# Cross attention's value product: probabilities stationary, value columns moving

## What is computed

```python
def _attn(q, k, v):
    s = jnp.einsum('bhqd,bhkd->bhqk', q, k) * SCALE
    p = jax.nn.softmax(s, axis=-1)
    return jnp.einsum('bhqk,bhkd->bhqd', p, v)
...
ctx = _attn(qT, k.transpose(0, 2, 1, 3), v.transpose(0, 2, 1, 3))
ctx_dca = _attn(qT, k_dca.transpose(0, 2, 1, 3), v_dca.transpose(0, 2, 1, 3))
ctx = ctx + DCA_WEIGHT * ctx_dca
return ctx @ Wo + bo
```

## Time and profile before

| | |
|---|---|
| median of 3 runs | 1019.32 us (1016.58 to 1019.96) |
| the profiled execution | 1017.64 us |
| its span, first to last instruction | 1015.9 us |
| mean granted clock of PE over the span | 0.832 |
| PE busy | 675.2 us (66%) |
| DVE busy | 728.4 us (72%) |
| ACT busy | 331.4 us (33%) |

### The profile page before, as it was taken

How to read it: one execution, slowest core, us unless ns; L and a number is a source line. 1 busy time by engine, 2 the same in 40 slices (tenths; PEclk the granted TensorE clock), 3 DMA queues, 4 the chain that set the end, 5 groups by cost and what they waited for, 6 DMA issues and landing times. The chain is left out here.

```text
span 1015.9 us, 9504 instructions
## 1 busy us (share of the span) xinstructions
PE 675.2 (66%) x3066; PEld 442.1 (44%) x3069; DVE 728.4 (72%) x1418; ACT 331.4 (33%) x530; POOL 193.8 (19%) x167
## 2 busy tenths in 40 slices
PE   4418986777777354349963454999990344389997
PEld 2304543343343243335742243556550123277775
DVE  5987798999999767659653783766429886944554
ACT  4004424525350133122302324555530222423231
POOL 0000002212222000034352940000003132203342
PEclk9759999999999776569986855999995575569999
DMA  9200004555555840323632000000005000000000
GB/s 243 76 12 0 1 0 78 87 94 93 97 90 97 206 128 1 124 62 108 133 92 87 0 1 0 1 2 1 1 1 207 0 1 0 10 0 1 20 3 21
DMA packets 35746, 55.27 MB, mean 54 GB/s; under 512 B 4578, under 2 KB 23658, under 8 KB 34418
## 3 DMA queue, kind: packets, MB, share of 16 engines
q0 software_dynamic: 10960, 22.94, 12.5%
q1 hardware_dynamic: 24738, 31.73, 10.2%
HBM read 31.73 MB, written 6.16 MB: 37 GB/s over the span
## 5 line engine op out<-in xcount | busy, mean ns | idle before, releaser
L499 PE MATMUL ps<-hT,regA 128*128 128x512 f32 x256 | 116.8, 599 | 1.3 <-ACT hT L424 1.3
L669 POOL DMA_DIRECT2D yssm<-regB x32 | 38.7, 1210 | 294.6 <-DVE regB L621 210.8
L613 DVE TENSOR_TENSOR_SCAN regB<-regB 128x512 f32<-128x512 f32 x64 | 74.9, 1212 | 5.0 <-DVE regB L608 0.5
L510 PE MATMUL ps<-regA,regC 128*128 128x256 f32 x256 | 64.8, 398 | 20.5 <-DVE regC L628 17.2
L1914 PE MATMUL ps<-regC 128*34 128x256 f32 x256 | 68.2, 389 | 11.6 <-ACT regC L1794 11.6
L499 PEld LDWEIGHTS ps<-hT,regA 128*128 128x128 f32 x256 | 49.2, 193 | 52.2 <-issue 47.7
L510 PEld LDWEIGHTS ps<-regA,regC 128*128 128x128 f32 x256 | 49.7, 199 | 39.8 <-DVE regC L628 27.1
L434 ACT ACTIVATE regC<-ps 128x512 f32<-128x512 f32 x32 | 19.1, 597 | 138.1 <-PE ps L499 138.0
L1128 POOL TENSOR_TENSOR w_lo<-regA,w_hi 128x768 fp32r<-128x768 f32 x22 | 42.4, 1932 | 100.3 <-ACT w_hi L1090 100.3
L1352 POOL DMA_INDIRECT regA<-h_rows,regA x31 | 29.5, 951 | 137.4 <-DVE regA L1572 107.1
L1266 DVE TENSOR_TENSOR regB<-regB,ps 128x512 f32<-128x512 f32 x22 | 15.1, 687 | 45.9 <-ACT regB L1108 45.9
(11 more groups left out here) (365 smaller groups left out, 1701.7 us busy)
## 6 DMA issues: line engine op xcount, KB each, us to landing
yssm<-regB POOLq DMA_DIRECT2D x32, 512.0 KB, 5.0
regB<-in_L_w SPq DMA_DIRECT2D x4, 1088.0 KB, 12.1
regA<-in_L_w SPq DMA_DIRECT2D x1, 4224.0 KB, 14.9
y_rows<-regA SPq DMA_DIRECT2D x31, 128.0 KB
regB<-in_L_w SPq DMA_DIRECT2D x1, 2176.0 KB, 13.1
regC<-in_L_W SPq DMA_DIRECT2D x2, 1024.0 KB, 5.7
x<-in_x SPq DMA_DIRECT2D x1, 1024.0 KB, 5.7
regB<-in_L_gate_pk SPq DMA_DIRECT2D x1, 1024.0 KB, 8.0
```

The lines of the kernel that those rows point to most:

```text
L499: m = nc.tensor.matmul(ps[:, 2 + 2 * (u % 2) + j, :], w[:, k * 2048 + c * P:k * 2048 + (c + 1) * P], hT[:, k, hf * HALF:(hf + 1) * HALF], ...
L510: m = nc.tensor.matmul(ps[:, t // 2, (t % 2) * D:(t % 2 + 1) * D], itm[:, u % 2, t * P:(t + 1) * P], WDv[:, c // 2, c % 2, :], start=(c == ...
L613: v.mark(nc.vector.tensor_tensor_scan(hs[:, k, :], dA[:, g % RD, k].rearrange("p b l -> p (b l)"), dBu[:, k, :], 0.0, ALU.mult, ALU.add))
L669: nc.gpsimd.dma_start(y, hc[:, g % 2], accum_op=ALU.add).then_inc(s_y, 16)
```

## The change

In `values(n)` the operands change places. For each of the two query tiles `qt` and the two key tiles `kt` a 128 keys x 128 queries block of `prob` is stationary, and the 34 columns of `vaug` move. The result has the queries on the partitions at once, in the layout that `normalize` reads. `evacuate_values` (the ACT copy), `turn_values` (the four turns), the tile `pvT` and the semaphores `s_pe` and `s_pt` go; `normalize` waits for `s_pv`.

```diff
-                    def evacuate_values(j):
-                        act.wait_ge(s_pv, j + 1)
-                        if j >= 2:
-                            act.wait_ge(s_pt, j - 1)
-                        nc.scalar.copy(pvT[0:VW, j % 2, :], ps[0:VW, 6 + j % 2, :]).then_inc(s_pe, 1)
...
-                        for kt in range(2):
-                            m = nc.tensor.matmul(ps[0:VW, 6 + j % 2, (n % 2) * S:(n % 2 + 1) * S], vaug[:, 2 * b + kt, hd, :],
-                                                 prob[:, n % 4, kt * S:(kt + 1) * S], start=kt == 0, stop=kt == 1)
+                        for qt in range(2):
+                            c0 = (2 * (n % 2) + qt) * VW
+                            for kt in range(2):
+                                m = nc.tensor.matmul(ps[:, 6 + j % 2, c0:c0 + VW],
+                                                     prob[:, n % 4, kt * S + qt * P:kt * S + (qt + 1) * P],
+                                                     vaug[:, 2 * b + kt, hd, :], start=kt == 0, stop=kt == 1)
                         if n % 2:
                             m.then_inc(s_pv, 1)
-
-                    def turn_values(j):
-                        pe.wait_ge(s_pe, j + 1)
-                        for i in range(4):
-                            m = nc.tensor.transpose(ps[:, 6 + j % 2, i * VW:(i + 1) * VW],
-                                                    pvT[0:VW, j % 2, i * P:(i + 1) * P], ident[0:VW, 0:VW])
-                        m.then_inc(s_pt, 1)
...
-                                if n >= 2 and n % 2 == 0:
-                                    turn_values(n // 2 - 1)
...
-                    turn_values(NHB // 2 - 1)
...
-                        dve.wait_ge(s_pt, j + 1)
+                        dve.wait_ge(s_pv, j + 1)
```

More of the change, by code:

```diff
@@ L1657, in stage4 @@
             rz = ar.take([8])
-            pvT = ar.take([2, 2 * S])
             nm = ar.take([2, 2, NH, 2])
@@ L1662, in stage4 @@
             (s_var, s_sd, s_h, s_hTp, s_hT, s_wk, s_w, s_v, s_q, s_qe, s_kv, s_kve, s_kb, s_qv, s_qs, s_sqi, s_sq, s_kp, s_qp, s_T, s_Te,
-             s_s1, s_mx, s_qm, s_s2, s_p, s_pv, s_pe, s_pt, s_o, s_oP, s_oT, s_fin, s_ctx, s_va) = (
-                sem("s4_" + n) for n in ("var sd h hTp hT wk w v q qe kv kve kb qv qs sqi sq kp qp T Te s1 mx qm s2 p pv pe pt o oP oT "
+             s_s1, s_mx, s_qm, s_s2, s_p, s_pv, s_o, s_oP, s_oT, s_fin, s_ctx, s_va) = (
+                sem("s4_" + n) for n in ("var sd h hTp hT wk w v q qe kv kve kb qv qs sqi sq kp qp T Te s1 mx qm s2 p pv o oP oT "
                                          "fin ctx va").split())
@@ L1806, in _ @@
                                 exponent(n)
-                            if n >= 2 and n % 2 == 0:
-                                evacuate_values(n // 2 - 1)
                             for i, first in enumerate((TK, TQ, TM)):
```

## The result

The changed kernel is slower: a median of 1072.06 us over four runs (1060.87 to 1081.75), against 1019.64 (1016.58 to 1020.2) for the kernel before; the ratio is 1.048, with a 95% interval of 1.040 to 1.057. Ratios leave out executions over 1.5% above the shortest of the same kernel, here the one of 1081.75 us. The forecast was 1038 with a range of 1022 to 1070; the median lies 2 us above that range. The direction was right, the size was not: +52 us instead of +20.

A forecast was written before the change was run, and what follows sets the result against it. The prediction took PE's own sequence to set the attention loop's pace. Its terms, 15 (last batch) + 4.5 (batches 0 to 2) + 0.8 (after the loop) = +20.3 us on 1017.64, gave 1038 us, range 1022 to 1070.

The forecast's parts named there:

- The removed turns and copy, -9.4 us: Attention loop: 32 groups of turns at 0.26 us saved (-8.3), plus the uncovered last copy and turns at loop end (-1.1).
- The new product costs at full clock what the old did, 0.98 us: Value product, per head: eight load-and-multiply pairs at 0.107 us plus 0.028 and a 0.10 gap make 0.98 us, as before.
- The clock falls in the last batch, +15 us: Last batch, only scores and product: clock falls some 3 us in; 14 heads lose 1.08 us each, net +15 us.
- Batches 0 to 2, +4.5 us: Batches 0 to 2: turns saved -6.2, low clock between batches +5.3, one failed block of turns +5.4; sum +4.5 us.
- A failed block of turns, +5.4 us, taken once: Batches 0 to 2: a block failing to raise the clock leaves three further heads and another block low, about 5.4 us.
- After the loop, +0.8: After the attention loop: last copy and turns saved, -1.1 us; line 173's turns and product with `Wo` starting low, +1.9.
- the +1.9: After the loop: line 173's turns and the first part of the product with `Wo` start from a low clock, +1.9 us.
- The forecast's own sign of being wrong: Attention loop: the prediction is wrong if the loop lasts under 130 us or over 175.
- (1): Attention loop: the clock holds, so only the savings count, -9.4 us, 1008 us; chance 0.15.
- (3): Value product: moving columns don't hide under loads, +22 us on the forecast, 1060, up to 1080; chance 0.06.
- (4): Clock lost only in part of the last batch, never between batches: 1018 to 1026 us; chance 0.07.
- (2): The clock stays low throughout the attention loop, +86 us, 1104 us; chance 0.04.

The follow-up runs named there:

- Three copies: Changed kernel, but every value-product multiplication moves the 34 columns three times over (102, the last 68 results unused), same loads; everywhere: 1009.58 us, 0.991 of the kernel before.
- the kernel with 32 added turns: Against the changed kernel with 102 moving columns in the last batch alone (1078.3 us): 32 unread turns added after that batch's first product; 1059.13 us.

## Why the prediction was wrong in size

- *The removed turns and copy, -9.4 us.* Right: 8.7 us by experiment.
- *The new product costs at full clock what the old did, 0.98 us.* Nearly: a head takes 1.44 us (the products at 635.47 and 636.91 in the changed kernel's timeline) against a forecast of 1.40, which is 0.04 x 64 = 2.6 us. Three copies take 1.50.
- *The clock falls in the last batch, +15 us.* Right: from the batch's first product to the end of the last one are 39.7 us (779.21 to 818.87) instead of 23.9 (726.75 to 750.66), +15.8. The forecast's 2.62 us a head at low clock measured 2.57. In the profiled execution the batch was entered at low clock already, so that all 16 heads were low and not 14.
- *Batches 0 to 2, +4.5 us.* This is the step that failed. It read "Between the last turns of a batch and the first of the next lie 5.2 us with scores and products alone. There I take one and a half heads at low clock", and so left slots 4 to 12 at full clock. The profiled execution lost 16.0, 17.5 and 16.2 us in the three batches, from the starts of their first products: 50 us. In batch 1 slots 5 to 11 took 3.00 us each instead of some 1.77, 7 x 1.23 = 8.6 us, and with slots 4 and 12 some 10 of the 17 us are there. Over the three batches slots 4 to 12 lost 30 of the 50 us (77.5 us against 47.6), where the forecast had nothing; the other 20 lie in the heads and turns around them. By the two experiments with three copies in and outside of slots 4 to 12, these slots and what follows from them are worth 33 us (1072.1 - 1039.5) and 37 us (1046.8 - 1009.6). The forecast had reasoned from the last batch because it has no other work. It did not ask whether a maxima group, which takes PE 0.34 us of a slot (743.82 to 744.16), is enough other work to keep the clock; the trace shows that the clock fell there.
- *A failed block of turns, +5.4 us, taken once.* It occurs more often than that. The blocks at 681.56 and 769.87 took 3.65 us at low clock, and left it low: the product behind the first took 1.92 us, the two products behind the second 3.62 together. In the one at 637.83 the clock was not low before, it fell there: it took 3.02 us, begun at full clock and ended at low, and the product in slot 3 that followed took 1.92 us. How often a block fails varies: the changed kernel's runs spread over 21 us, those with three copies over 2.5. PE's timeline of the changed kernel, the blocks at 637.83 and 681.56 (line 1849):

```profile
637.83 3.02 PE L1849 MATMUL ps<-ident,regA 128*128 128x128 f32 x16
640.77 0.79 PE L1891 MATMUL ps<-q4T,k4T 52*128 52x256 f32 x2
641.50 1.92 PE L1907 MATMUL ps<-regC 128*128 128x34 f32 x8
...
681.56 3.65 PE L1849 MATMUL ps<-ident,regA 128*128 128x128 f32 x16
685.14 0.79 PE L1891 MATMUL ps<-q4T,k4T 52*128 52x256 f32 x2
685.87 1.92 PE L1907 MATMUL ps<-regC 128*128 128x34 f32 x8
```

- *After the loop, +0.8.* The last copy and turns went (from the last product's end at 818.87 to the division at 818.91 there is nothing), but the +1.9 did not come. It supposed that the turns of `o` had run at full clock before. Most of them had not: the clock fell during them (0.59 from 753 to 754 us, 0.50 from 754 to 756), and they took 3.23 us, against 3.45 now. In the kernel with three copies everywhere and in the one without copy and turns, where the clock stayed at 1.00, they take 1.97. The product with `Wo` takes 7.17 us as before. The step came to about -0.9.

The forecast's own sign of being wrong was a loop of over 175 us. It lasted 189.2 (629.71 to 818.87).

The rivals: the clock did not hold (1); the moved columns do hide (3); it was lost in more than the last batch (4). It did not stay low throughout (2), since 12 of the 48 heads of batches 0 to 2 ran at full clock; but that rival, at 1104 us and with a chance of 0.04, is about as near to the measured 1072 as the forecast of 1038, and the chance was too small. Two places of the Trainium skill's page "TensorE: Matmul & The Clock Gate" bear on this. Its advice under "Why this matters for your kernels", keep TensorE busy without gaps for full clock, is not enough here: PE was busy for 3.00 of 3.00 us in each of the three stretches from 741 to 750 us, while the clock fell from 1.00 to 0.50. And its section "Part 4: PE-mode transpose", by which transposes don't count for the clock, is contradicted by the kernel with 32 added turns: the same batch without them stayed at 0.50 for 42 us, and with them the clock rose while they ran.

Not settled: why a given block of sixteen turns raises the clock or doesn't, and why the clock can even fall in one (637.83). The copies move more columns and also write more results; no experiment tells the two apart. Nor was anything varied in the maxima group itself (the reductions' pace, the blocks of 48 rows).

## What to carry to other kernels

Before exchanging stationary and moving operand, look at what the stretch does to the matrix engine's clock and not only at what its instructions take: an exchange that is even in time at full clock and saves the turns besides (0.8%) cost 5% here, because the clock fell with 34 moving columns behind each load, where 102 kept it. The sign is a duration that grows in instructions nobody touched, beside a granted clock under 1.00 at a busy PE. Where loads set the pace, moving more columns behind them is nearly free (0.06 us a head) and bought the clock back: 1009.6 us against 1072.1.

## What the runs showed of the hardware

- What a form of work does to the clock depends on the level at which it starts. Eight pairs a head with 102 moving columns held 1.00 for the whole last batch in one kernel and left 0.50 at 0.50 for the whole batch in another; 32 turns in front of it made the difference (2.69 us a head without, 1.50 with them).
- A movement of up to 102 columns, the most that was tried, hides under the next load of 128 columns in float32: 1.08 us for eight pairs with 34 columns, 1.14 with 102.
- A granted clock between the two levels in a stretch of some us, as the 0.57 of a batch, is a mixture: the eight pairs took 1.08 or 1.92 us, and only a group in which the clock changed lay between (1.51 us at 730.19).
